# Attention by probabilities times (values times output weights), made per pair of heads and passed through DRAM

## What is computed

```python
q = (layernorm(x) @ Wq).reshape(b, n, 8, 64)
k = (context @ Wk).reshape(b, m, 8, 64)
v = (context @ Wv).reshape(b, m, 8, 64)
attn = softmax(einsum('bihd,bjhd->bhij', q, k) * 64 ** -0.5)
out = einsum('bhij,bjhd->bihd', attn, v).reshape(b, n, 512) @ Wout + bout
x = x + tanh(g_xattn) * out
```

## Time and profile before

| | |
|---|---|
| median of three runs | 973.93 us (973.85 to 975.16) |
| the profiled execution | 973.07 us, span 971.2 us |
| busy share of the span | TensorE 94%, its weight load 87%, VectorE 84%, ScalarE 54%, GpSimd 51% |
| mean granted clock | 0.974 |

### The profile page before, as it was taken

How to read it: one execution, slowest core, us unless ns; L and a number is a source line. 1 busy time by engine, 2 the same in 40 slices (tenths; PEclk the granted TensorE clock), 3 DMA queues, 4 the chain that set the end, 5 groups by cost and what they waited for, 6 DMA issues and landing times. The chain is left out here.

```text
span 971.2 us, 20907 instructions
## 1 busy us (share of the span) xinstructions
PE 914.7 (94%) x6722; PEld 849.8 (87%) x6722; DVE 814.2 (84%) x1928; ACT 524.3 (54%) x1191; POOL 495.3 (51%) x605
## 2 busy tenths in 40 slices
PE   6699999999999999999979999999779999999996
PEld 5599999999999999998867888888659999699996
DVE  7899999999999999998749888888738788378885
ACT  6477777776777676554344555554214444144442
POOL 5345345364535535434443555555416766546776
PEclk9699999999999999999989999999979999999998
DMA  8213233223322332544351444444268999388892
GB/s 243 75 48 100 57 92 107 76 79 95 104 61 84 108 86 89 159 151 145 107 185 66 164 168 170 165 164 142 88 226 283 339 346 339 134 287 267 259 288 79
DMA packets 108341, 151.14 MB, mean 156 GB/s; under 512 B 21830, under 2 KB 72394, under 8 KB 108240
## 3 DMA queue, kind: packets, MB, share of 16 engines
q1 hardware_dynamic: 92880, 107.60, 36.7%
q0 software_dynamic: 15360, 42.24, 11.3%
HBM read 90.19 MB, written 65.90 MB: 161 GB/s over the span
## 5 line engine op out<-in xcount | busy, mean ns | idle before, releaser
L681 POOL TENSOR_TENSOR prob<-prob,row_sum 128x616 f32<-128x616 f32 x64 | 77.9, 1218 | 142.3 <-DVE row_sum L905 142.3
L1126 POOL DMA_INDIRECT rows_scratch<-row,slot x64 | 67.9, 1062 | 75.0 <-DVE row L1379 60.4
L1532 POOL DMA_INDIRECT rows_scratch<-prow x80 | 78.7, 984 | 51.5 <-issue 30.5
L1532 POOL DMA_INDIRECT out<-prow x80 | 78.7, 984 | 48.1 <-issue 27.1
L1642 ACT ACTIVATE eyT_hi<-ps_ey 128x512 fp32r<-128x512 f32 x80 | 47.9, 598 | 92.3 <-PE ps_ey L1554 91.4
L75 PE MATMUL ps_h<-w_flat,eyT_hi 128*128 x320 | 96.6, 302 | 0.0
L76 PE MATMUL ps_h<-w_flat,eyT_hi 128*128 x320 | 89.8, 281 | 0.0
L77 PE MATMUL ps_h<-w_flat,eyT_lo 128*128 x320 | 89.8, 281 | 0.0
L75 PE MATMUL ps_s<-M_hi,xT_hi 128*128 128x308 f32 x256 | 81.9, 320 | 7.5 <-PEq L387 4.1
L817 ACT ACTIVATE prob<-prob,rstd 128x616 f32<-128x616 f32 x64 | 51.9, 811 | 67.3 <-DVE prob L895 67.3
L261 POOL TENSOR_TENSOR xT_lo<-xT_raw,xT_hi 128x512 fp32r<-128x512 f32 x32 | 41.1, 1286 | 88.5 <-ACT ctxb_hi L227 87.4
(11 more groups left out here) (297 smaller groups left out, 3346.3 us busy)
## 6 DMA issues: line engine op xcount, KB each, us to landing
prow<-rows_scratch SPq DMA_DIRECT2D x160, 258.0 KB, 4.0
rows_scratch<-blank SPq DMA_DIRECT2D x34, 258.0 KB, 4.4
xT_raw<-in_xT SPq DMA_DIRECT2D x32, 256.0 KB, 4.5
x_tok<-in_x SPq DMA_DIRECT2D x32, 256.0 KB, 2.9
x_scratch<-x_tok SPq DMA_DIRECT2D x32, 256.0 KB, 3.2
row<-x_scratch SPq DMA_DIRECT2D x16, 512.0 KB, 3.9
x_ahead<-in_x SPq DMA_DIRECT2D x26, 256.0 KB, 4.4
w_raw<-in_W SPq DMA_DIRECT2D x16, 256.0 KB, 3.5
```

Of the source, the lines that this page charges most:

```text
L681: nc.gpsimd.tensor_tensor(pr, pr, row_sum[i][:, :].unsqueeze(2).broadcast_to((P, H, CK)), ALU.mult).then_inc(normed, 1)
L1126: pool.indirect_dma_start(c.rows1, bass.IndirectOffsetOnAxis(slot1[:, t:t + 1], 0), row[G % NX][:, i, :], None).then_inc(scattered[G % NX] ...
L1532: pool.indirect_dma_start(dram, bass.IndirectOffsetOnAxis(target, 0), row[u][:, i, 0:columns], None, bounds_check=bound, oob_is_err=False) ...
```

## The change

Values are no longer made per batch. `values(n)` makes vT for one pair of heads over the four batches of a group (308 columns), n = 0 to 31, four pairs a group. `project_part(n, m)` multiplies it at once by that pair's rows of Wout, for 103, 103 and 102 of the 308 context rows, 4 matmuls of 256 columns each. ScalarE copies each part to one of two stage buffers (`copy_part`), and SP stores it in a DRAM scratch, each part in two transfers since it crosses a batch (`store_part`; the pieces have 77, 26, 51, 52, 25 and 77 rows, of two heads). `load_vw` loads the 616 rows of one batch (8 heads by 77) as chunks of 128, 128, 128, 128 and 104; GpSimd splits them (`split_vw`). The probabilities are transposed in the same chunks, 10 transposes for 16, and `attend_out` multiplies PT by VW: 5 chunks by 3 products by 2 halves, 30 matmuls, with the residual right behind. OT and `project_out` are gone. Five pairs (14 of their 15 parts) are made ahead of the loop; in batch b the pair b + 5. Wout is held for each head twice, in both halves of the partitions. x is updated in place.

```diff
+CHUNKS = -(-HK // P)
+LAST_ROWS = HK - (CHUNKS - 1) * P
+PARTS = ((0, 103), (103, 206), (206, GK))
+UNITS = B
+AHEAD = GB + 1
...
-                high(nc, c.wo_hi[:, :, :], wo_raw[:, :, :], w_hi)
+                for at in (0, 1):
+                    for j in range(2):
+                        high(nc, head_rows(c.wo_hi, j, j ^ at), wo_raw[half(j), :, :], w_hi)
...
+                for j in range(2):
+                    nc.gpsimd.tensor_tensor(head_rows(c.wo_lo, j), wo_raw[half(j), :, :], f32(head_rows(c.wo_hi, j)),
+                                            ALU.subtract).then_inc(wo_lo_done, 1)
+                    pool.wait_ge(wo_lo_done, j + 1)
...
+        def made_in(b):
+            return b + AHEAD if 0 <= b and b + AHEAD < UNITS else None
...
+                def store_part(n, m):
+                    lo, hi = PARTS[m]
+                    i, pair = (3 * n + m) % 2, n % GB
+                    sp.wait_ge(part_copied, 3 * n + m + 1)
+                    for q in range(lo // CK, (hi - 1) // CK + 1):
+                        first, last = max(lo, q * CK), min(hi, (q + 1) * CK)
+                        sp.dma_start(c.vw[GB * (n // GB) + q, 2 * pair:2 * pair + 2, first - q * CK:last - q * CK, :]
+                                     .rearrange("h k d -> k h d"),
+                                     stage[i][first - lo:last - lo, :, :]).then_inc(part_out[i], 16)
+                def load_vw(b):
+                    wait(sp, vw_lo, b)
+                    for i in range(2):
+                        sp.wait_ge(part_out[i], 16 * 2 * 6 * (b // GB + 1))
+                    rows = c.vw[b].rearrange("h k d -> (h k) d")
+                    whole = (CHUNKS - 1) * P
+                    sp.dma_start(vw_raw[:, 0:CHUNKS - 1, :], rows[0:whole, :].rearrange("(c p) d -> p c d", p=P)
+                                 ).then_inc(vw_in, 16)
+                    sp.dma_start(vw_raw[0:LAST_ROWS, CHUNKS - 1, :], rows[whole:HK, :]).then_inc(vw_in, 16)
...
+                        if made_in(b - 1) or b == 0:
+                            store_part(b - 1 + AHEAD, 2)
+                        if b + 1 < B:
+                            load_vw(b + 1)
                         if not (first and q == 0):
                             store(b - 1, nxt)
-                groups(sp, body)
-                sp.wait_ge(c.blank_made, 3)
+                        if n:
+                            store_part(n, 0)
+                        if not (last and q == GB - 1):
+                            wait(sp, x1_stats, 2 * b)
+                            wait(sp, x1_out[nxt], 16 * ((b + 1) // 2))
+                            load_x(sp, c, a, b + 1, nxt)
+                        if n:
+                            store_part(n, 1)
+                for n in range(AHEAD):
+                    for m in range(2 if n == AHEAD - 1 else 3):
+                        store_part(n, m)
+                    if n == GB - 1:
+                        sp.wait_ge(vw_clean, 1)
+                        load_vw(0)
+                groups(body)
...
+                def split_vw(b):
+                    pool.wait_ge(vw_in, 32 * (b + 1))
+                    wait(pool, out_done, 2 * (b - 1))
+                    hi, lo = VW[b % 2]
+                    nc.gpsimd.tensor_copy(hi[:, :, :], vw_raw[:, :, :]).then_inc(vw_hi, 1)
+                    pool.wait_ge(vw_hi, b + 1)
+                    nc.gpsimd.tensor_tensor(lo[:, :, :], vw_raw[:, :, :], f32(hi[:, :, :]),
+                                            ALU.subtract).then_inc(vw_lo, 1)
                 def body(g, first, last):
                     for q in range(GB):
                         b, par, nxt = GB * g + q, q % 2, (q + 1) % 2
+                        if q == GB - 1 and exists(g + 2):
+                            split_group(nc.gpsimd, pool, a, g + 2)
+                        if b > 0:
+                            split_vw(b)
+                        norm(b, 0)
                         if not (last and q == GB - 1):
                             split_batch(nc, pool, a, b + 1, nxt)
-                        norm(b, 0)
-                        if q == GB - 1 and exists(g + 2):
-                            split_group(nc.gpsimd, pool, a, g + 2)
...
                         norm(b, 1)
+                        if b == 0:
+                            split_vw(b)
...
-                def attend_values(b):
...
-                def project_out(b):
...
-                def make_V(b, par, m_units):
...
+                def values(n):
+                    wait(pe, part_copied, 3 * n - (0 if n >= AHEAD else 3))
+                    wait(pe, vT_lo, 2 * n - 2)
+                    of_context(nc, c.wv_hi, c.wv_lo, context(a, n // GB), value_bank(n), n % GB, vT_done)
+                def project_part(n, m):
+                    lo, hi = PARTS[m]
+                    pe.wait_ge(vT_lo, 2 * n + 2)
+                    wait(pe, part_copied, 3 * n + m - (1 if n < AHEAD else 0))
+                    bank = part_bank(n, m)
+                    for j in range(2):
+                        h, out = 2 * (n % GB) + j, bank[0:hi - lo, j, :]
+                        nc.tensor.matmul(out, vT[j][:, lo:hi], c.wo_hi[:, h, :], start=True, stop=False)
+                        last = nc.tensor.matmul(out, vT[j][:, lo:hi], c.wo_lo[:, h, :],
+                                                start=False, stop=True)
+                    last.then_inc(part_done, 1)
+                def attend_out(b, i):
+                    if i == 0:
+                        pe.wait_ge(PT_lo, 3 * b + 3)
+                        pe.wait_ge(vw_lo, b + 1)
+                    wait(pe, x1_done, 2 * b + i)
+                    hi, lo = VW[b % 2]
+                    tokens = slice(i * P, (i + 1) * P)
+                    rows = [P] * (CHUNKS - 1) + [LAST_ROWS]
+                    products(nc, ps_o[:, i, :], [
+                        (PT[0][0:r, k, tokens], PT[1][0:r, k, tokens], hi[0:r, k, :], lo[0:r, k, :])
+                        for k, r in enumerate(rows)]).then_inc(out_done, 1)
                 def transpose_probs(b, i):
                     pe.wait_ge(normed, 2 * b + i + 1)
-                    for j in range(2):
...
+                    wait(pe, PT_lo, 3 * b)
+                    for k in range(CHUNKS - 1):
+                        last = nc.tensor.transpose(ps_pt[i][:, k * P:(k + 1) * P], prob[i][:, k * P:(k + 1) * P],
+                                                   c.ident[:, :])
+                    last.then_inc(PT_done, 1)
+                def transpose_rest(b):
+                    pe.wait_ge(PT_lo, 3 * b + 1)
+                    for i in range(2):
+                        last = nc.tensor.transpose(rest_bank[:, i * P:(i + 1) * P], prob[i][:, (CHUNKS - 1) * P:HK],
+                                                   c.ident[:, :])
+                    last.then_inc(PT_done, 1)
...
                 def body(g, first, last):
                     for q in range(GB):
                         b = GB * g + q
+                        n = made_in(b)
                         pe.wait_ge(a.x_split, b + 1)
                         if q == 0:
                             pe.wait_ge(a.M_lo, 2 * H * (g + 1))
                         scores(b, g, q, 0)
                         if not last:
-                            wait(pe, V_lo, 0 if first and q == 0 else b)
                             make_M_units(b, q, 0)
-                        if not (first and q == 0):
-                            attend_values(b - 1)
+                        if made_in(b - 1) or b == 0:
+                            project_part(b - 1 + AHEAD, 2)
+                        if b > 0:
+                            attend_out(b - 1, 0)
                         scores(b, g, q, 1)
+                        if n:
+                            if q == GB - 1:
+                                pe.wait_ge(a.ctx_split, g + 3)
+                            values(n)
+                        if b > 0:
+                            attend_out(b - 1, 1)
                         if not last:
                             make_M_units(b, q, 1)
                         transpose_probs(b, 0)
-                        if not (first and q == 0):
-                            project_out(b - 1)
-                        if makes_K(g, q):
-                            if q == GB - 1:
-                                pe.wait_ge(a.ctx_split, g + 3)
-                            make_K(nc, pe, c, a, b + GB + 1, (q + 1) % GB)
-                        make_V(b, q % 2, 2 * H * GROUPS if last else 2 * H + 4 * b + 3)
+                        if n:
+                            project_part(n, 0)
+                            make_K(nc, pe, c, a, n)
+                            project_part(n, 1)
                         transpose_probs(b, 1)
-                groups(pe, body)
+                        transpose_rest(b)
+                for n in range(AHEAD):
+                    values(n)
+                    for m in range(2 if n == AHEAD - 1 else 3):
```

(34 more changed lines are left out.)

255 lines of the change are left out of this document (117 added, 138 removed).

## The result

The changed kernel takes 1007.55 us (median of 4 runs, 1005.18 to 1009.69) where the kernel before takes 974.21 (973.85 to 975.16): a ratio of 1.034, 95% interval 1.0315 to 1.0365. It is slower, as forecast, but by 33.3 us and not 17.9, and just above the upper end of the range. The profiled execution of the changed kernel has a span of 1007.9 us and a mean granted clock of 0.947 (before: 971.2 and 0.974). Two executions in what follows, one of e3 (1039.07 us) and one of e11 (2096.05 us), ran in another, slower state and are left out of the medians; the one of e11 is the profiled one, so there is no trace of e11 to set beside the others.

A forecast was written before the change was run, and what follows sets the result against it. TensorE was taken as the bound, VectorE close behind. The longer start, batches of 13.1 us, six boundaries and last batches move attention's end from 493.04 to 511 us; +17.9 on the 973.93 median gives 992 us, range 974 to 1006.

The forecast's parts named there:

- main price: Start of attention: five pairs made before the first scores, which move from 33.6 to 76.0 us, 42 us later.
- signs by which the forecast would be wrong: First scores starting before 65 us, or batches taking under 12.4 us.
- The new wait: Attention loop: TensorE waits 0.71 us for prob at the second transposes, so a batch takes 12.38 + 0.71 = 13.1 us.
- Ends of groups: After each of the first six groups, GpSimd's extra work lengthens the batch by 1.05 us, 6.3 us in all.
- The last batches: Last four batches, without M or new pairs: VectorE's chain sets the pace at 11.8 us each.
- GpSimd's copy: Copy of VW to fp32r at the head of each batch: 1.8 us taken, range 1.1 to 2.96.
- The rival of a dear copy: GpSimd's copy takes 2.96 us: boundaries cost 6.9 more, first batches 2.3, total 1001 us; chance 0.14.
- The start: Before the first scores: attention starts at 38.3 us, first part copied from 45.8, then four pairs of 7.4 each.
- the estimated 3 us of cost: Start: if fewer DMA engines doubled the middle part's store time, its buffer comes free 0.7 us late in four pairs.
- Batch 1: Its VW loads only after batch 0's split, at 94.3 us; some 6 us longer than the next batch.
- Late loads: VW landing takes over 7.6 us, for instance behind blank-row writes: +1.4 us in each of 8 batches, 1003; chance 0.08.
- The rest of the program: Everything behind the end of attention was taken as the same, a change of 0 us.

The follow-up runs named there:

- e3: Changed kernel with VectorE taking the second two M_lo subtractions ahead of the sums, the residual left in place: 1008.10 us.
- e11: e10 plus the edits of e1, e6 and e7, and VectorE's first chain of scales behind the first vT subtractions: 971.8 us, ratio 0.9949 to 0.9981.
- e1: Changed kernel with the loop's keys in the other ps_proj bank, so they wait for the first M_lo subtraction instead of the second: 999.13 us.
- e2: Changed kernel with the second half's sums and M_lo ahead of the residual on VectorE: 1007.54 us.
- e8: e2 plus SP issuing the next batch's x_ahead load about half a batch earlier, behind the load of VW: 992.66 us.
- e10: e8 plus GpSimd splitting VW ahead of a later group's context at the last batch of a group: 985.67 us.
- e6: Changed kernel with the parts of the first four pairs going through three stage buffers instead of two: 1003.33 us.
- e7: Changed kernel with GpSimd splitting VW of batch 0 ahead of the first normalization instead of behind the second: 1002.68 us.
- e9: Changed kernel with SP's blank-row writes of the last two groups moved behind the load of VW and the store of x: 1006.05 us.
- e13: Kernel before with one more 20 MB scratch tensor in DRAM, between its two other scratch tensors: 975.22 us, ratio 0.9987 to 1.0022.

## Why the prediction was right and wrong

The direction held, by the forecast's own main price: five pairs in series ahead of the first scores put the first row_max at 73.24 us instead of 39.25, while batches 2 to 26 gained only 8.0 us (345.0 instead of 353.0). The size did not hold, and none of the signs by which the forecast would be wrong came: first scores at 70.8 us, batches above 12.4. First row_max of a batch, forecast (start of the batch and 2.0) and measured:

| stretch | forecast us | measured us | difference |
|---|---|---|---|
| to row_max of batch 0 | 78.0 | 73.24 | -4.8 |
| batches 0 and 1 | 33.3 | 34.25 | +1.0 |
| batches 2 to 26 | 333.8 | 345.0 | +11.2 |
| batches 27 to 30 | 47.6 | 50.4 | +2.8 |
| batch 31 to the end of attention | 18.3 | 19.3 | +1.0 |
| rest of the program, by the medians | 0 | 4.1 | +4.1 |

**The step that failed is "The new wait".** Its prices for TensorE's work are right (12.43 us a batch for 12.38), and VectorE's chain to the sums and the end of the normalization too: forecast 5.94 after the scores, measured 269.90 - 263.90 = 6.0 (from the first matmul of the values). But it has the keys without a wait, and puts the wait at the second transposes, for prob. That M_lo moved behind the sums stood in the rows of the order; I followed VectorE's chain to the normalization and not to the other reader of VectorE's work in that stretch, the bank that the keys need. The prediction's own terms would have given it: the sum at 3.6, 0.95 for it and its reciprocal and 0.85 for both M_lo make 5.4 us after the scores, where the keys are due at 0.71 + 1.86 + 0.57 + 0.40 + 0.49 = 4.0. That is a wait of 1.4 us, and 12.38 + 1.4 = 13.8 us a batch. Measured, the keys wait 1.36 us, the transposes come 1.3 us behind that, and an ordinary batch takes 13.6 to 13.8 instead of 13.1. e1 and e3 show the place; e2 and e8 show that ScalarE's load of x_ahead stands right behind it.

**Ends of groups.** The cost was put at 1.05 us over an ordinary batch, in the batch behind a group, from GpSimd's 15 small steps. It came at another place: the last batch of a group takes 14.1 us, 0.4 over ordinary ones, which were longer than forecast; over those of e8 it is 1.1, and 0.7 in the first. e10 takes away all of the 1.1 and half of the 0.7. So most of it is a wait that the sum has not: GpSimd's for ScalarE's ctxM_hi, ahead of the split. Some 0.4 us is left to the small steps.

**The last batches.** The 11.8 us of these were VectorE's chain alone, with no term for TensorE's clock. Batches 27 and 30 took 12.0 and 11.9 us, but 28 and 29 13.7 and 13.0 at a granted clock of 0.87 and 0.89. From row_max of batch 31 to the end of attention it is 19.3 us in the six traces with a granted clock of 0.91 there, the changed kernel's among them, and 17.6 in the five with 0.97 to 0.99. So most of the +2.8 and +1.0 of the table goes with the clock; that is read from the rows, and no run tested it.

**GpSimd's copy** took 1.25 us, not 1.8; 1.1 was the lower end. The subtraction took 2.95 (2.96). The estimate of 1.1 us by the Trainium skill, GPSIMD Engine Reference, section 3.1, was the nearer one here. The page gives the 1.03 cycles an element to loop bodies with k ≤ 2, bound by the read and write ports; that a copy is one of them is the prediction's reading. The rival of a dear copy is refuted; a cheaper copy left less to the ends of groups.

**The start** was 4.8 us shorter than forecast. The first part was copied at 43.83 us and not 45.8, since attention began 2 us earlier than forecast (VectorE's chain at 36.34, not 38.3). A pair took 7.1, 6.6, 6.3 and 6.3 us, not 7.4: the store that is waited for landed 3.3, 2.8, 2.6 and 2.6 us after its copy, and not 3.8. That these two terms were too dear is luck for the forecast: with the right ones it would have been some 5 us lower, and further off.

The stores of 51 and 52 rows were never waited for in the changed kernel: their buffer's next copy, at 50.92 and so on, waited for TensorE. They do land later: in e6 one was waited for (0.16 us), 4.5 us after its copy (57.66 to 62.12), where those of 77 and 26 rows took the 2.6 to 3.3 us above. The trace of the changed kernel agrees with the rule for which the prediction cited the Trainium skill, DMA: Bandwidth & Descriptors, section "Why a DMA increments its semaphore by 16 and not by 1": it records 16 landings for the two transfers of 51 and 52 rows (3 and 13 engines by the rule) and 24 for those of 77 and 26 (11 and 13). But in the changed kernel the buffer had 5.6 us until its next copy (45.28 to 50.92), so the estimated 3 us of cost did not come.

**Batch 1** waited for its VW as forecast (e7). **Late loads** of VW, a rival, are there at the end: GpSimd waited 2.86 and 1.23 us, where the rival had 1.4 in each of eight batches. But in the changed kernel they did not set a batch, and the rival is not what made the time longer (e9).

**The rest of the program** was taken as unchanged. Its code is, but from the end of attention to the end of the span it took 478.2 us in the profiled execution before and 485.6 after. In the other profiles of changed kernels it took 478.1 to 485.0, its second half (the passes) alone 253.5 to 260.6, and the kernel before has 254.5 in one profile and 256.4 in e13. So most of the 7.4 us of these two profiles is spread between executions; whether some 3 us of it belong to the change stays open, and e13 rules out only the added tensor. Without these 4.1 us the time would lie inside the range, and without the 11.2 us of batches 2 to 26, where the failed step lies, as well.

## What to carry to other kernels

Where an engine's own order changes, follow every reader of what has moved back, not only the chain one has in mind: a bank that is not yet read out holds the next writer as an unfinished sum holds the softmax, and the later of the two sets the pace. When a shorter chain gains little, look at the engine between (here ScalarE, held by a load that has nothing to do with the chain) before calling the chain wrong. A change that adds a serial start can still be worth it if the steady loop is freed of its waits: here 1007.6 became 971.8 us with nearly the same work in another order, 0.35% below the kernel before.
